# A transformer block with two-pass attention on one core: splits taken from the banks, five units turned by transfers, an update moved to GpSimd

## The chip, the cores and the metric

One NeuronCore of a Trainium2 chip runs the kernel. The metric is the device time of one execution in microseconds, the median of several.

## The reference

Two sequences (batch elements) of 1024 tokens with 256 features. `mod` gives shifts, scales and gates per batch element from a small vector.

```python
h = layernorm(x) * (1 + ca) + sa
Q, K, V = split(h @ c_attn_w + c_attn_b)               # 256 columns each
base = softmax(Q[:, :128] @ K[:, :128].T * 0.25)       # first softmax
ctx  = base @ V[:, :128]
bias = tanh(ctx * cam_gate) @ K[:, :128].T * (0.25 * sigmoid(w0 + 0.5 * w1))
attn = softmax(Q @ K.T * 0.25 + bias)                  # second softmax
x = x + ga * (attn @ V @ c_proj_w + c_proj_b)
h = layernorm(x) * (1 + cb) + sb
x = x + gb * (gelu(h @ proj1.T + b1) @ proj2.T + b2)
```

## The kernel before

Every fp32 product is made of three products of fp32r halves: a value is split into a high half (a copy to fp32r) and a low half (value minus high), and `mm3` (L199 to L203) does high x high, high x low and low x high. So each operand of TensorE costs a high copy and a subtraction, and the engines beside TensorE mostly make these.

The program is written out by hand: each engine has its own list in program order, and semaphores tie them together. An engine that waits holds everything behind it in its list.

For each batch element (b = 0, 1) attention goes in steps s = 0 to 17 over 16 units. A unit is 128 queries against all 1024 keys. Units 0 to 7 are the first softmax, with one 128-row chunk of features (6 matmuls of 512 columns). Units 8 to 15 are the second, with two chunks (12 matmuls). In step s TensorE makes the scores of unit s (`scores`), then turns the probabilities of unit s - 2 (`transpose_probs`, 8 transposes of 128x128, L1305), then does the step's fillers: value and query/key projections in steps 0 to 6, the context product of pair p (`cam_context`, units 2p and 2p + 1) in step 5 + 2p, and from step 11 the product with V (`attend`). Scores alternate between two double banks `s_ps`, so scores of unit u wait for the exp of unit u - 2.

A unit goes: scores; row maximum on VectorE (`row_max`, L904); exp and row sum on ScalarE (`softmax_exp`, L642) into one of three `prob` buffers; reciprocal on VectorE; in the first softmax a division on GpSimd (`divide_by_sum`, L441); the turn into one of two banks `t_ps`; high copy on ScalarE (`prob_high`, L627); low half on VectorE (`prob_low`, L898, pt_lo). The context product of a pair ends in tanh on ScalarE (`cam_tanh`), and `q_update` (L867 to L873, VectorE) adds the scaled tanh to the first query chunk and splits it again. Scores of units 8, 10, 12 and 14 wait for the updates 0, 1, 2 and 3.

Units 8 to 13 (`DMA_UNITS`) are not turned by TensorE. Exp writes them in another order, SyncE writes them to DRAM in four transfers and reads them back in one (a trip: `send_probs`, `write_rows` L349, `read_rows` L356), and VectorE transposes blocks of 32x32 into the bank (`turn_probs`, L882), in step u + 2. Four of the norms make the same trip. SyncE makes trips one after the other, and waits in each for its writes before it issues the read.

Queries and keys come from 8 jobs of 512 tokens (`QK_JOBS`). Each job's bank is copied once by ScalarE to f32s with scale and bias (`qk_bias`), and VectorE makes both halves from there (`qk_split`, L853 and L855), except in the first four jobs of b = 0, where ScalarE makes the high half too.

GpSimd further adds constants and the attention result to x (L459, L465), splits the feed-forward weights in steps 8 to 15 of b = 0 (`split_ffn`, L450), and takes the root for the norms (`inv_std`, L436).

Of the kernel before, what the change touches and what calls it, by code (L numbers as in the profile page):

```python
# [10 lines left out]
P = 128  # L11
# [14 lines left out]
TRIPS = ([("p", 0, u) for u in DMA_UNITS] + [("h", 0, 3), ("h", 1, 0), ("h", 1, 1)]  # L26
         + [("p", 1, u) for u in DMA_UNITS] + [("h", 1, 3)])
# [6 lines left out]
def adaln_block_kernel(nc, x, cols, wmod, w_attn, wv_t, wp, rows, w1_t, w2_t, out):  # L34
# [5 lines left out]
    with ctx:  # L40
# [118 lines left out]
        qk32_ready = lsem("qk32_ready", 8)  # L159
# [15 lines left out]
        qcam_ready = lsem("qcam_ready", T)  # L175
# [16 lines left out]
        probs_back = [sem(f"probs_back{d}") for d in range(2)]  # L192
# [39 lines left out]
        A_READ_OUT = {"v": vlo_ready, "qk": qk32_ready, "ctx": tanh_ready, "pv": o1_ready, "f2": t2_ready,  # L232
                      "wvp": wv_lo_ready, "gate": gate_copied, "row": row_added}

        T_JOBS = []
        for b in range(B):
            T_JOBS += [(b, "h", r) for r in range(4)]
            if b == 0:
                T_JOBS += [(0, "mod", 1)]
            T_JOBS += [(b, "p", n) for n in range(2 * UNITS)] + [(b, "h", r) for r in range(4, 8)]  # L240
# [8 lines left out]
        def read_out(jobs, signals, job):  # L249

            n = jobs.index(job)
            if n < 2:
                return None
            b, kind, k = jobs[n - 2]
            if (b, kind) == (0, "h") and k < 4:
                return hlo_ready, k // 2 * 2 + 2
            if kind == "h":
                return h32_ready, h_count(b, k)
            if kind == "mod":
                return mod_ready, 3  # L260
            s = signals[kind]
            return s, b * per.get(s, 0) + k + 1
# [22 lines left out]
        def slot(trip):  # L285

            d = trip[2] % 2
            same = [t for t in TRIPS[:TRIPS.index(trip) + 1] if t[2] % 2 == d]
            return d, same[-2] if len(same) > 1 else None, len(same)

# [18 lines left out]
        QK_JOBS = [(0, 0), (2, 0), (2, 1), (0, 1), (1, 0), (3, 0), (1, 1), (3, 1)]  # L309

# [3 lines left out]
        def _(sp):  # L314
# [27 lines left out]
            wait(sp, v_psum, 0, T)  # L342
            wait(sp, qk_psum, 0, 8)
            sp.dma_start(w1_raw[:, :, :], w1_t.rearrange("(c p) n -> p c n", p=P)).then_inc(w1_in, 16)
            sp.dma_start(w2_raw[:, :, :], w2_t.rearrange("(c p) n -> p c n", p=P)).then_inc(w2_in, 16)
# [6 lines left out]
            def read_rows(k):  # L352
# [3 lines left out]
                sp.dma_start(quad[:, d, :], turned[k, :, :, :, :].rearrange("q c i n -> (q c) (i n)"))\  # L356
# [12 lines left out]

            def send_norm(b, n):  # L370
# [5 lines left out]
                if kind == "p":  # L376
                    wait(sp, t_psum, ob, 2 * o + 2)
# [4 lines left out]
            for b in range(B):  # L382
                for u in DMA_UNITS:
# [12 lines left out]
        def _(pool):  # L396
# [35 lines left out]
            def inv_std(b, n):  # L432
# [3 lines left out]
                G.tensor_tensor(rstd[:, h], ve[:, h], minus_half[:, :], ALU.pow).then_inc(rstd_ready[n // 2], 1)  # L436

# [77 lines left out]
            for b in range(B):  # L515
                for s in range(UNITS):
                    if s < T:
# [14 lines left out]
                    if s == UNITS - 1:  # L532
                        inv_std(b, 2)
# [20 lines left out]
        def _(act):  # L554
# [43 lines left out]
            def qk_bias(b, j):  # L598
                m, h = QK_JOBS[j]
                wait(act, qk_psum, b, j + 1)  # L600
                if j >= 3:
                    wait(act, qklo_ready, b, j - 2)
                src = s_bank(j) if j < 4 else a_bank(b, "qk", j)[:, :]
                if m < 2:
                    a = A(f32s[:, j % 3, :], src, ACT.Identity, scale=QSCALE, bias=bq_scaled[:, m:m + 1])
                else:
                    a = A(f32s[:, j % 3, :], src, ACT.Identity, bias=cols_sb[:, C_BK + m - 2:C_BK + m - 1])
                a.then_inc(qk32_ready, 1)

            def qk_high(j):  # L610

                m, h = QK_JOBS[j]
                scale, bias = (QSCALE, bq_scaled[:, m:m + 1]) if m < 2 else (1.0, cols_sb[:, C_BK + m - 2:C_BK + m - 1])
                A((q_hi if m < 2 else k_hi)[:, m % 2, h * HALF:(h + 1) * HALF], s_bank(j), ACT.Identity,
                  scale=scale, bias=bias).then_inc(qkhi_ready, 1)
# [4 lines left out]

            def prob_high(b, u):
                for g in range(2):
                    wait(act, t_psum, b, 2 * u + g + 1)
# [7 lines left out]
            def softmax_exp(b, u):  # L631
# [3 lines left out]
                if u - 3 in DMA_UNITS:  # L635
                    act.wait_ge(probs_out, sent("p", b, u - 3))
                elif u >= 3:
                    wait(act, t_psum, b, 2 * (u - 2))
                dst, src = prob[:, u % 3, :], s_ps[u % 2][:, :]
                if u in DMA_UNITS:  # L640
# [37 lines left out]
            qk_bias(0, 0)  # L678
            v_high(0, 0)
            qk_high(0)  # L680
            v_high(0, 1)
            qk_bias(0, 1)
            v_high(0, 2)
            qk_high(1)
# [4 lines left out]
            for b in range(B):  # L689
                if b == 0:  # L690
                    qk_bias(0, 2)
                    qk_high(2)
                    qk_bias(0, 3)
                    qk_high(3)
                    copy_gates()
                else:
                    for j in range(1, 4):
                        qk_bias(b, j)
                        v_high(b, j - 1)
                for s in range(UNITS + 2):  # L700
                    if s - 2 in DMA_UNITS and s < UNITS - 1:
                        softmax_exp(b, s)
                    if s >= 2:
# [5 lines left out]
                    if s < UNITS:  # L709
                        for kind, k in fillers(b, s):  # L710
                            if kind == "v" and s >= 2:
                                v_high(b, k)
                            if kind == "qk":
                                qk_bias(b, k)
# [13 lines left out]
                if b + 1 < B:  # L728
                    qk_bias(b + 1, 0)
# [5 lines left out]
        def _(dve):  # L735
# [43 lines left out]

            def qk_low(j):  # L780
                m, h = QK_JOBS[j]
                hi, lo = (q_hi, q_lo) if m < 2 else (k_hi, k_lo)
                dst = (slice(None), m % 2, slice(h * HALF, (h + 1) * HALF))
                wait(dve, qk32_ready, 0, j + 1)
                wait(dve, qkhi_ready, 0, j + 1)
                V.tensor_tensor(lo[dst], f32s[:, j % 3, :], f(hi[dst]), ALU.subtract).then_inc(qklo_ready, 1)
# [61 lines left out]
            def qk_split(b, j):  # L848
                m, h = QK_JOBS[j]
                hi, lo = (q_hi, q_lo) if m < 2 else (k_hi, k_lo)  # L850
                dst = (slice(None), m % 2, slice(h * HALF, (h + 1) * HALF))
                wait(dve, qk32_ready, b, j + 1)
                V.tensor_copy(hi[dst], f32s[:, j % 3, :]).then_inc(qkhi_ready, 1)  # L853
                wait(dve, qkhi_ready, b, j + 1)
                V.tensor_tensor(lo[dst], f32s[:, j % 3, :], f(hi[dst]), ALU.subtract).then_inc(qklo_ready, 1)  # L855
# [5 lines left out]

            def q_update(b, p):

                dst = (slice(None), 0, slice(2 * P * p, 2 * P * (p + 1)))
                t = th[:, p % 2, :]
                wait(dve, tanh_ready, b, p + 1)
                V.scalar_tensor_tensor(t, t, lw_scaled[:, :], f(q_lo[dst]), ALU.mult, ALU.add).then_inc(qcam_ready, 1)  # L867
                wait(dve, qcam_ready, b, 2 * p + 1)
                V.tensor_tensor(t, t, f(q_hi[dst]), ALU.add).then_inc(qcam_ready, 1)
                wait(dve, qcam_ready, b, 2 * p + 2)  # L870
                V.tensor_copy(q_hi[dst], t).then_inc(qphi_ready, 1)
                wait(dve, qphi_ready, b, p + 1)
                V.tensor_tensor(q_lo[dst], t, f(q_hi[dst]), ALU.subtract).then_inc(qplo_ready, 1)  # L873
# [581 lines left out]
```

## Time and profile before

| | us |
|---|---|
| median of 3 runs (lowest, highest) | 305.36 (304.52, 306.32) |
| the profiled execution, its own time | 304.42 |
| its span | 302.5 |
| TensorE busy in it | 297.4 |
| VectorE, ScalarE, GpSimd busy | 226.3, 157.9, 106.8 |
| transfers | 27.08 MB, mean 90 GB/s |

The span is the time from the first to the last instruction on the engines. Busy times count an instruction from its start to its end. Matmuls are pipelined, so that the duration of one overlaps the next. In the rows, PE is TensorE, DVE VectorE, ACT ScalarE, POOL GpSimd and SPq the queue that SyncE issues transfers to.

### The profile page before, as it was taken

How to read it: one execution, taken by the hardware profiler on the slowest of the kernel's cores; microseconds unless marked ns; L12 is line 12 of the kernel's file. 1: busy time of each engine (PE TensorE's matmuls, PEld its weight loads, DVE VectorE, ACT ScalarE, POOL GpSimd, SP SyncE). 2: the span in 40 equal slices, each digit the busy share in tenths (PEclk: the TensorE clock that was granted, in tenths of full speed). 3: DMA queues.
4: the chain of work that ended last, by engine and by line, in shares of the span. 5: the costliest groups of instructions: out<-in, count | busy, mean ns of one | idle time of the engine just before them, and what ended most of it. 6: DMA issues, size and time to landing. Idle time of an engine off the chain costs nothing.

```text
span 302.5 us, 5086 instructions
## 1 busy us (share of the span) xinstructions
PE 297.4 (98%) x1888; PEld 270.2 (89%) x1888; DVE 226.3 (75%) x448; ACT 157.9 (52%) x268; POOL 106.8 (35%) x130
## 2 busy tenths in 40 slices
PE   8999999999999999999999999999999999999995
PEld 7889888898998988998998888898998999899895
DVE  4796789896899979768964789786889994944521
ACT  2676766463344447617733577554262445923920
POOL 3436743244456548027021141330011344314110
PEclk9999999999999999999999999999999999999999
DMA  6920200726665000451231000005656300141001
GB/s 223 378 96 1 56 17 0 279 69 205 213 194 154 3 0 2 139 175 35 72 106 36 0 2 0 2 0 136 212 161 215 112 1 2 24 134 53 0 20 52
DMA packets 19544, 27.08 MB, mean 90 GB/s; under 512 B 1984, under 2 KB 16064, under 8 KB 19520
## 3 DMA queue, kind: packets, MB, share of 16 engines
q1 hardware_dynamic: 19520, 26.76, 28.2%
q8 instruction: 15, 0.25, 0.3%
q14 instruction: 9, 0.07, 0.1%
HBM read 15.74 MB, written 10.49 MB: 87 GB/s over the span
## 4 chain that ended last, share of the span: by engine, by line
PE 89%; DVE 5%; ACT 2%; issue 2%; POOL 1%; DVEq 0%; POOLq 0%
PE a_ps L203 14%; PE a_ps L201 13%; PE a_ps L202 13%; PE s_ps L201 12%; PE s_ps L203 12%; PE s_ps L202 12%; PE t_ps L1305 5%; PE s_ps L1134 2%; DVE nmax L904 2%; DVE pt_lo L898 1%; ACT prob L642 1%; PE t_ps L1230 1%; ACT pt_hi L627 1%; PE s_ps L1160 1%; PE s_ps L1169 1%
## 5 line engine op out<-in xcount | busy, mean ns | idle before, releaser
L642 ACT ACTIVATE prob<-s_ps,nmax 128x1024 f32<-128x1024 f32 x32 | 35.8, 1118 | 48.4 <-DVE nmax L904 48.3
L904 DVE TENSOR_REDUCE nmax<-s_ps 128x1 f32<-128x1024 f32 x32 | 38.9, 1217 | 11.8 <-PE s_ps L203 11.6
L627 ACT ACTIVATE pt_hi<-t_ps 128x512 fp32r<-128x512 f32 x64 | 34.9, 595 | 23.9 <-PE t_ps L1305 19.4
L898 DVE TENSOR_TENSOR pt_lo<-t_ps,pt_hi 128x512 fp32r<-128x512 f32 x64 | 41.0, 683 | 3.8 <-ACT pt_hi L627 3.7
L201 PE MATMUL s_ps<-k_hi,q_hi 128*128 128x512 f32 x96 | 38.0, 396 | 0.0
L203 PE MATMUL s_ps<-k_hi,q_lo 128*128 128x512 f32 x96 | 37.6, 392 | 0.0
L202 PE MATMUL s_ps<-k_lo,q_hi 128*128 128x512 f32 x96 | 37.5, 391 | 0.0
L201 PE MATMUL a_ps<-v_hi,pt_hi 128*128 128x256 f32 x128 | 36.4, 284 | 0.0
L203 PE MATMUL a_ps<-w_hi,pt_lo 128*128 128x256 f32 x128 | 36.2, 283 | 0.0
L201 PE MATMUL a_ps<-w_hi,pt_hi 128*128 128x256 f32 x128 | 36.2, 283 | 0.0
L202 PE MATMUL a_ps<-w_lo,pt_hi 128*128 128x256 f32 x128 | 36.2, 283 | 0.0
L203 PE MATMUL a_ps<-v_hi,pt_lo 128*128 128x256 f32 x128 | 35.8, 280 | 0.0
L202 PE MATMUL a_ps<-v_lo,pt_hi 128*128 128x256 f32 x128 | 35.8, 279 | 0.0
L441 POOL TENSOR_SCALAR prob<-prob,rinv 128x1024 f32<-128x1024 f32 x16 | 18.3, 1145 | 48.8 <-DVE rinv L908 48.7
L933 DVE TENSOR_TENSOR pt_lo<-prob,pt_hi 128x512 fp32r<-128x512 f32 x32 | 23.3, 753 | 11.5 <-ACT pt_hi L665 11.4
L306 POOL TENSOR_TENSOR x_all<-x_all,o 128x256 f32<-128x256 f32 x15 | 11.1, 739 | 55.9 <-DVE o L928 55.9
L465 POOL TENSOR_TENSOR x_all<-x_all,o 128x256 f32<-128x256 f32 x16 | 11.8, 738 | 49.6 <-DVE o L919 49.6
L662 ACT ACTIVATE prob<-s_ps,cols_sb 128x512 f32<-128x512 f32 x32 | 22.0, 687 | 13.4 <-PE s_ps L203 13.3
L201 PE MATMUL s_ps<-ht_hi,w_hi 128*128 128x512 f32 x64 | 25.1, 392 | 0.0
L202 PE MATMUL s_ps<-ht_lo,w_hi 128*128 128x512 f32 x64 | 24.9, 390 | 0.0
L203 PE MATMUL s_ps<-ht_hi,w_lo 128*128 128x512 f32 x64 | 24.9, 389 | 0.0
L202 PEld LDWEIGHTS a_ps<-w_lo,pt_hi 128*128 128x128 f32 x128 | 24.6, 192 | 0.2
(166 smaller groups left out, 756.3 us busy)
## 6 DMA issues: line engine op xcount, KB each, us to landing
f32s<-turned SPq DMA_DIRECT2D x16, 512.0 KB, 3.5
turned<-prob SPq DMA_DIRECT2D x48, 128.0 KB, 2.9
w_raw<-w_t SPq DMA_DIRECT2D x2, 1024.0 KB, 6.2
turned<-xn SPq DMA_DIRECT2D x16, 128.0 KB, 2.4
out<-x_all SPq DMA_DIRECT2D x16, 128.0 KB, 1.7
x_all<-x SPq DMA_DIRECT2D x3, 512.0 KB, 10.0
wmod_raw<-wmod SPq DMA_DIRECT2D x1, 1024.0 KB, 8.8
wmod_raw<-wmod SPq DMA_DIRECT2D x2, 256.0 KB, 4.6
```

Of the source, the lines that this page charges most:

```text
L201: nc.tensor.matmul(o, st_hi, mv_hi, start=first, stop=False)
L202: nc.tensor.matmul(o, st_hi, mv_lo, start=False, stop=False)
L203: return nc.tensor.matmul(o, st_lo, mv_hi, start=False, stop=last)
L441: G.tensor_scalar(prob[:, u % 3, :], prob[:, u % 3, :], rinv[:, u:u + 1], 1.0, ALU.mult, ALU.mult).then_inc(pnorm_ready, 1)
L465: G.tensor_tensor(xt, xt, o1[:, t % 2, :], ALU.add).then_inc(x2_ready, 1)
L627: A(pt_hi[:, (u // 2) % 2, 4 * g:4 * g + 4, (u % 2) * P:(u % 2 + 1) * P], t_bank(b, "p", 2 * u + g)[:, :].rearrange("p (t n) -> p t n", n= ...
L642: A(dst, src, ACT.Exp, bias=nmax[:, u:u + 1], accum_out=rsum[:, u:u + 1]).then_inc(exp_ready, 1)
L662: A(gelu_of(n), s_bank(n % 4), ACT.Gelu, bias=cols_sb[:, C_B1 + n % HC:C_B1 + n % HC + 1]).then_inc(gelu_ready, 1)
L898: V.tensor_tensor(pt_lo[dst], t_bank(b, "p", 2 * u + g)[:, :].rearrange("p (t n) -> p t n", n=P), f(pt_hi[dst]), ALU.subtract).then_inc(pt ...
L904: V.tensor_reduce(nmax[:, u:u + 1], s_ps[u % 2][:, :], AX.X, ALU.max, negate=True).then_inc(nmax_ready, 1)
L933: V.tensor_tensor(gt_lo[:, n % HC, :], gelu_of(n), f(gt_hi[:, n % HC, :]), ALU.subtract)\
L1305: last = nc.tensor.transpose(t_bank(b, "p", 2 * u + g)[:, t * P:(t + 1) * P], prob[:, u % 3, c:c + P], ident[:, :])
```

## The change

- `by_dma`, `DMA_CAM`: units 4 and 6 of b = 0 and 2, 4 and 6 of b = 1 of the first softmax make the trip too, after their division. They land in xn, and VectorE's turn, the high copy and the low half come at the end of step u + 3. The order in which units go through the turning banks changes accordingly (`turn_order`: 5 before 4, 7 before 6, 3 before 2).
- `qk_copies`, `qk_low`: ScalarE makes the high half of every job straight from the bank. For queries it also makes the fp32 copy, from which VectorE takes the low half; for keys VectorE takes the low half straight from the bank (`scalar_tensor_tensor`: bank + bias - high). No high copy is left on VectorE.
- `q_update` runs on GpSimd, as five instructions, ahead of the division of its step.
- The two loads of the feed-forward weights are issued by ScalarE in step 6 of b = 0 (`load_ffn`), not by SyncE.
- In step 15 GpSimd takes the root (`inv_std(b, 2)`) before its two additions, not after.

```diff
+DMA_CAM = ((4, 6), (2, 4, 6))
+TRIPS = ([("p", 0, u) for u in (*DMA_CAM[0], *DMA_UNITS)] + [("h", 0, 3), ("h", 1, 0), ("h", 1, 1)]
+         + [("p", 1, u) for u in (*DMA_CAM[1], *DMA_UNITS)] + [("h", 1, 3)])
...
+        def turn_order(b):
+            order = list(range(UNITS))
+            for u in DMA_CAM[b]:
+                order[u], order[u + 1] = u + 1, u
+            return order
...
+        def landing(d):
+            return xn[:, :, :].rearrange("p t e -> p (t e)") if d == 2 else quad[:, d, :]
...
             def send_probs(b, u):
                 k = TRIPS.index(("p", b, u))
-                wait(sp, exp_ready, b, u + 1)
+                wait(sp, pnorm_ready if u < T else exp_ready, b, u + 1)
                 write_rows(k, prob[:, u % 3, :])
-                if u - 2 in DMA_UNITS:
-                    wait(sp, t_psum, b, 2 * (u - 2) + 2)
-                else:
+                if by_dma(b, u - 2) and u not in (T, T + 1):
+                    wait(sp, t_psum, b, turned_by(b, u - 2))
+                elif u >= T:
                     wait(sp, qklo_ready, b, 8)
+                elif b == 0:
+                    wait(sp, ht_psum, 0, 4)
                 read_rows(k)
...
+            def q_update(b, p):
+                dst = (slice(None), 0, slice(2 * P * p, 2 * P * (p + 1)))
+                t = th[:, p % 2, :]
+                wait(pool, tanh_ready, b, p + 1)
+                G.tensor_scalar(t, t, lw_scaled[:, :], 1.0, ALU.mult, ALU.mult).then_inc(qcam_ready, 1)
+                wait(pool, qcam_ready, b, 3 * p + 1)
+                G.tensor_tensor(t, t, f(q_lo[dst]), ALU.add).then_inc(qcam_ready, 1)
+                wait(pool, qcam_ready, b, 3 * p + 2)
+                G.tensor_tensor(t, t, f(q_hi[dst]), ALU.add).then_inc(qcam_ready, 1)
+                wait(pool, qcam_ready, b, 3 * p + 3)
+                G.tensor_scalar(q_hi[dst], t, 1.0, 1.0, ALU.mult, ALU.mult).then_inc(qphi_ready, 1)
+                wait(pool, qphi_ready, b, p + 1)
+                G.tensor_tensor(q_lo[dst], t, f(q_hi[dst]), ALU.subtract).then_inc(qplo_ready, 1)
...
                 for s in range(UNITS):
+                    for kind, p in fillers(b, s - 1):
+                        if kind == "ctx":
+                            q_update(b, p)
                     if s < T:
                         divide_by_sum(b, s)
...
+                    if s == UNITS - 1:
+                        inv_std(b, 2)
                     if s >= 10:
                         attn_const(b, s - 10)
                     if s >= 11:
                         attn_residual(b, s - 11)
-                    if s == UNITS - 1:
-                        inv_std(b, 2)
...
+            def qk_copies(b, j):
                 m, h = QK_JOBS[j]
                 wait(act, qk_psum, b, j + 1)
                 src = s_bank(j) if j < 4 else a_bank(b, "qk", j)[:, :]
+                dst = (slice(None), m % 2, slice(h * HALF, (h + 1) * HALF))
                 if m < 2:
+                    if j >= 3:
+                        wait(act, qklo_ready, b, j - 2)
+                    A(f32s[:, j % 3, :], src, ACT.Identity, scale=QSCALE, bias=bq_scaled[:, m:m + 1]).then_inc(q32_ready, 1)
+                    A(q_hi[dst], src, ACT.Identity, scale=QSCALE, bias=bq_scaled[:, m:m + 1]).then_inc(qkhi_ready, 1)
                 else:
+                    A(k_hi[dst], src, ACT.Identity, bias=cols_sb[:, C_BK + m - 2:C_BK + m - 1]).then_inc(qkhi_ready, 1)
...
                 for s in range(UNITS + 2):
                     if s - 2 in DMA_UNITS and s < UNITS - 1:
                         softmax_exp(b, s)
-                    if s >= 2:
+                    if s >= 2 and not (s - 2 < T and by_dma(b, s - 2)):
                         prob_high(b, s - 2)
...
+                    if b == 0 and s == 6:
+                        load_ffn()
+                    if s - 3 < T and by_dma(b, s - 3):
+                        prob_high(b, s - 3)
...
+            def qk_low(b, j):
                 m, h = QK_JOBS[j]
                 dst = (slice(None), m % 2, slice(h * HALF, (h + 1) * HALF))
                 wait(dve, qkhi_ready, b, j + 1)
+                if m < 2:
+                    wait(dve, q32_ready, b, Q_JOBS.index(j) + 1)
+                    V.tensor_tensor(q_lo[dst], f32s[:, j % 3, :], f(q_hi[dst]), ALU.subtract).then_inc(qklo_ready, 1)
+                else:
+                    src = s_bank(j) if j < 4 else a_bank(b, "qk", j)[:, :]
+                    V.scalar_tensor_tensor(k_lo[dst], src, cols_sb[:, C_BK + m - 2:C_BK + m - 1], f(k_hi[dst]),
+                                           ALU.add, ALU.subtract).then_inc(qklo_ready, 1)
...
-                    for kind, k in fillers(b, s - 1):
-                        if kind == "ctx":
-                            q_update(b, k)
...
+                    if s - 3 < T and by_dma(b, s - 3):
+                        turn_probs(b, s - 3)
+                        prob_low(b, s - 3)
...
-                    if s >= 2 and s - 2 not in DMA_UNITS:
+                    if s >= 2 and not by_dma(b, s - 2):
                         transpose_probs(b, s - 2)
```

## Rows read from the trace of the kernel before

**Rows 1.** The page's first part: busy us, share of the span, instructions.
```profile
PE 297.4 (98%) x1888; PEld 270.2 (89%) x1888; DVE 226.3 (75%) x448; ACT 157.9 (52%) x268; POOL 106.8 (35%) x130
```

**Rows 2.** Waits of PE: us in total, times, longest.
```profile
PE t_ps L1230 <- DVE pt_lo L898: 0.6, 1, 0.6
```

**Rows 3.** Windows: us, busy (instructions), clock, transfers; then chain: start, us, what.
```profile
67.78:109.40 41.62, 41.03 (x282) 37.76 (x281) 35.04 (x69) 16.57 (x32) 22.70 (x27) 1.00 0.45 140
...
81.81 1.24 DVE nmax L904
```

**Rows 4.** The chain, step 7 of the first element.
```profile
54.36 0.87 PE t_ps L1305 x8
```

**Rows 5.** Lines by form: shapes, count, busy us, mean ns, idle before.
```profile
L1305 PE MATMUL t_ps<-ident,prob 128*128 128x128 f32 x160 | 20.7, 273 | 0.0
...
L882 DVE STREAM_TRANSPOSE t_ps<-f32s 128x512 f32<-128x512 f32 x32 | 21.0, 701 | 0.0
...
L853 DVE CAST q_hi<-f32s 128x512 fp32r<-128x512 f32 x6 | 4.0, 664 | 2.3 <-ACT f32s L605 2.3
...
L459 POOL TENSOR_TENSOR x_all<-x_all,consts 128x256 f32<-128x256 f32 x16 | 11.8, 737 | 0.0
...
L450 POOL TENSOR_SCALAR w_hi<-w_raw 128x512 fp32r<-128x512 f32 x8 | 5.0, 620 | 16.2 <-DVE nmax L904 16.2
```

**Rows 6.** SyncE's queue: start, us, issue; then part 6: median us to landing.
```profile
53.48 0.47 SPq L345 DMA_DIRECT2D w_raw<-w_t  x1
63.39 1.80 SPq L349 DMA_DIRECT2D turned<-prob  x4
67.18 0.34 SPq L356 DMA_DIRECT2D f32s<-turned  x1
...
f32s<-turned SPq DMA_DIRECT2D x16, 512.0 KB, 3.5
```

**Rows 7.** Timeline, steps 6 and 7 of the first element.
```profile
49.35 0.56 ACT L649 ACTIVATE th<-a_ps,gate_bias,cols_sb 128x256 f32<-128x256 f32 x1 [0.52 <-PE a_ps L203]
...
53.64 1.28 POOL L441 TENSOR_SCALAR prob<-prob,rinv 128x1024 f32<-128x1024 f32 x1 [3.98 <-DVE rinv L908]
53.97 1.23 DVE L869 TENSOR_TENSOR th<-th,q_hi 128x256 f32<-128x256 f32 x1
```

**Rows 8.** Windows (PE, PEld, DVE, ACT, POOL) from score start to score start: steps 6, 7, 9, 10.
```profile
49.15:52.81 3.66, 3.66 (x23) 3.09 (x21) 3.56 (x5) 2.20 (x4) 0.52 (x1) 1.00 0.00 0
52.81:57.81 5.00, 5.00 (x40) 4.69 (x38) 4.64 (x9) 2.21 (x5) 1.28 (x1) 1.00 0.67 246
...
61.34:67.78 6.44, 6.44 (x47) 5.91 (x46) 6.11 (x11) 4.13 (x7) 2.79 (x4) 1.00 0.32 81
67.78:70.52 2.74, 2.74 (x15) 2.26 (x14) 0.31 (x2) 0.75 (x3) 1.03 (x1) 1.00 0.82 257
```

**Rows 9.** One query update's window, DVE on th alone; then the tile view (min/median/max ns).
```profile
216.50:218.40 1.90, 1.62 (x4) 1.00 0.90 284
...
L869 DVE TENSOR_TENSOR th<-th,q_hi x8: 424/426/1241, 54.0 to 228.2; 128x256 f32<-128x256 f32 x8
```

**Rows 10.** Timeline, steps 14 to 17 of the first element.
```profile
92.50 0.39 PE L203 MATMUL s_ps<-k_hi,q_lo 128*128 128x512 f32 x1
...
93.27 1.21 DVE L904 TENSOR_REDUCE nmax<-s_ps 128x1 f32<-128x1024 f32 x1
...
103.14 0.94 DVE L816 TENSOR_SCALAR ve<-mv 128x4 f32<-128x4 f32 x1
103.99 1.28 DVE L898 TENSOR_TENSOR pt_lo<-t_ps,pt_hi 128x512 fp32r<-128x512 f32 x2
...
104.71 0.73 POOL L465 TENSOR_TENSOR x_all<-x_all,o 128x256 f32<-128x256 f32 x1
105.40 1.04 POOL L436 TENSOR_TENSOR rstd<-ve,minus_half 128x4 f32<-128x4 f32 x1
106.48 1.80 DVE L835 TENSOR_SCALAR xn<-x_all,mv,rstd 128x256 f32<-128x256 f32 x4 [1.14 <-POOL rstd L436]
108.53 0.28 PE L203 MATMUL a_ps<-v_hi,pt_lo 128*128 128x256 f32 x1
109.42 0.30 PE L1230 MATMUL t_ps<-ident,xn 128*128 128x128 f32 x1 [0.61 <-DVE pt_lo L898]
```

More of the change, by code:

```diff
@@ L191, in adaln_block_kernel @@
         probs_out = sem("probs_out")
-        probs_back = [sem(f"probs_back{d}") for d in range(2)]
+        probs_back = [sem(f"probs_back{d}") for d in range(3)]
         def wait(eng, s, it, k):
@@ L239, in adaln_block_kernel @@
                 T_JOBS += [(0, "mod", 1)]
-            T_JOBS += [(b, "p", n) for n in range(2 * UNITS)] + [(b, "h", r) for r in range(4, 8)]
+            T_JOBS += [(b, "p", 2 * u + g) for u in turn_order(b) for g in range(2)] + [(b, "h", r) for r in range(4, 8)]
         T_READ_OUT = {"p": ptlo_ready}
@@ L261, in read_out @@
             s = signals[kind]
-            return s, b * per.get(s, 0) + k + 1
+            if kind == "qk" and QK_JOBS[k][0] >= 2:
+                s = qklo_ready
+            return s, b * per.get(s, 0) + (turned_by(b, k // 2, k % 2) if kind == "p" else k + 1)
         def v_bank(b, t):
@@ L285, in slot, with home, by_dma @@
         def slot(trip):
-            d = trip[2] % 2
-            same = [t for t in TRIPS[:TRIPS.index(trip) + 1] if t[2] % 2 == d]
+            def home(t):
+                return 2 if t[0] == "p" and t[2] < T else t[2] % 2
+            d = home(trip)
+            same = [t for t in TRIPS[:TRIPS.index(trip) + 1] if home(t) == d]
             return d, same[-2] if len(same) > 1 else None, len(same)
+        def by_dma(b, u):
+            return ("p", b, u) in TRIPS
+        def landing(d):
+            return xn[:, :, :].rearrange("p t e -> p (t e)") if d == 2 else quad[:, d, :]
         def gelu_of(n):
@@ L309, in adaln_block_kernel @@
         QK_JOBS = [(0, 0), (2, 0), (2, 1), (0, 1), (1, 0), (3, 0), (1, 1), (3, 1)]
+        Q_JOBS = [j for j in range(8) if QK_JOBS[j][0] < 2]
         block = ctx.enter_context(nc.Block())
@@ L355, in read_rows @@
                 sp.wait_ge(probs_out, 16 * Q * (k + 1))
-                sp.dma_start(quad[:, d, :], turned[k, :, :, :, :].rearrange("q c i n -> (q c) (i n)"))\
+                sp.dma_start(landing(d), turned[k, :, :, :, :].rearrange("q c i n -> (q c) (i n)"))\
                     .then_inc(probs_back[d], 16)
@@ L376, in send_norm @@
                 if kind == "p":
-                    wait(sp, t_psum, ob, 2 * o + 2)
+                    wait(sp, t_psum, ob, turned_by(ob, o))
                 else:
@@ L382, in _ @@
             for b in range(B):
-                for u in DMA_UNITS:
+                for u in (*DMA_CAM[b], *DMA_UNITS):
                     send_probs(b, u)
@@ L619, in v_high, with load_ffn @@
                 A(v_hi[:, t, :], v_bank(b, t)[:, 0:NV], ACT.Copy).then_inc(vhi_ready, 1)
+            def load_ffn():
+                wait(act, v_psum, 0, T)
+                wait(act, qk_psum, 0, 8)
+                nc.scalar.dma_start(w1_raw[:, :, :], w1_t.rearrange("(c p) n -> p c n", p=P)).then_inc(w1_in, 16)
+                nc.scalar.dma_start(w2_raw[:, :, :], w2_t.rearrange("(c p) n -> p c n", p=P)).then_inc(w2_in, 16)
             def prob_high(b, u):
                 for g in range(2):
-                    wait(act, t_psum, b, 2 * u + g + 1)
+                    wait(act, t_psum, b, turned_by(b, u, g))
                     if b == 0 and u == 0:
@@ L690, in _ @@
                 if b == 0:
[L691 to L694, printed above, removed]
+                    qk_copies(0, 2)
+                    qk_copies(0, 3)
                     copy_gates()
@@ L778, in h_low @@
                 V.tensor_tensor(ht_lo[dst], h32[:, r % 2, :], f(ht_hi[dst]), ALU.subtract).then_inc(hlo_ready, 1)
[L780 to L786, printed above, removed]
             def norm_stats(b, n):
@@ L860, in v_low @@
                     .then_inc(vlo_ready, 1)
[L862 to L873, printed above, removed]
             def turn(trip, kind, jobs, signal):
@@ L895, in prob_low @@
                 for g in range(2):
-                    wait(dve, pthi_ready, b, 2 * u + g + 1)
+                    wait(dve, pthi_ready, b, turned_by(b, u, g))
                     dst = (slice(None), (u // 2) % 2, slice(4 * g, 4 * g + 4), slice((u % 2) * P, (u % 2 + 1) * P))
@@ L1011, in _ @@
                         tile_stats(b, TH - 1)
-                    if s >= 2:
+                    if s >= 2 and not (s - 2 < T and by_dma(b, s - 2)):
                         prob_low(b, s - 2)
@@ L1281, in scores @@
                 if u == 1:
-                    wait(pe, qk32_ready if b else qkhi_ready, b, 4)
+                    wait(pe, qkhi_ready, b, 4)
                 if u >= 2:
```

64 lines of the change are left out of this document (21 added, 43 removed).

## The prediction

> **What bounds the kernel now.** First the page's busy times: TensorE is busy 297.4 of a span of 302.5 us, VectorE 75% [rows 1]. A share of 98% could still hide small bubbles, so next come TensorE's own waits: beside the first operand there is one, 0.6 us on VectorE's pt_lo [rows 2]. Apart from that wait, the start and the tail, the kernel goes as fast as TensorE takes its list. An edit is worth what it takes off that list, plus what it takes off that wait, minus new waits; work saved on the other engines is worth nothing in itself. The chain of waits seems to say otherwise, since it runs through VectorE and ScalarE from 81.8 to 109 us. But it is followed back from that one wait, and shows that this stretch has little room, not that it costs 27 us: TensorE is busy 41.03 of its 41.62 us, at its full 2.4 GHz [rows 3].
>
> **Term 1, five units by transfers.** TensorE turns a unit's probabilities with 8 transposes. The line view's mean of 273 ns for one [rows 5] is not the price, since matmuls overlap; the chain gives start to start 0.87 us for all 8 [rows 4], 109 ns each. Units 4 and 6 of the first batch element and 2, 4 and 6 of the second leave the list: 5 x 0.87 = 4.35 us. No other matmul is added, removed or reshaped, so this is gained in full unless a wait appears.
>
> Elsewhere it adds 5 x 2 block transposes of 0.70 us on VectorE [rows 5], 7.0 us in all, and 20 writes and 5 reads on SyncE. ScalarE's and VectorE's copies of such a unit stay, and come one step later. Is a turned unit there when it is wanted? A trip took 3.8 us from the first write's issue to the read's (63.39 to 67.18), and a read lands in 3.5 us [rows 6]: 7.3 us. Take unit 6 of the first element. Its division ran from 53.64 for 1.28 us [rows 7], so it is back at 62.2. Its turn stands at the end of step 9, which began at 61.34 [rows 8] and, with two pieces of 0.87 us gone before it, begins at 59.6. Scores 2.8 us (step 10, which is nothing else [rows 8]), row maximum 1.2 and the pt_lo of unit 7 1.3 [rows 10] put the turn at 64.9: 2.7 us in hand. The same count gives some 1.6 us for unit 6 of the second element, more for the others. A late trip holds VectorE at the turn, with the next row maximum behind it, then that unit's exp, then the scores two units on: some 4 us more pass before TensorE waits. I take 0, from 0 (nothing that TensorE waits for today gets faster by it) to 2 us lost.
>
> The steps also get shorter, and VectorE has least room in them: busy 3.56 of 3.66 us in step 6, 4.64 of 5.00 in step 7, 6.11 of 6.44 in step 9 [rows 8]. In step 6 it loses a pt_lo (1.3), the query update (1.62 [rows 9]) and the high copy (0.4 to 0.7), and keeps row maximum, reciprocal and one low half: 2.1 us in a step of 2.8. Step 7 then has a row maximum, two units' pt_lo, a turn and a reciprocal: 5.3 against 5.0, behind 0.7 to spare. Step 9 has the same 5.3 against 6.4. In all VectorE gets 7.0 us and loses 8 x 1.62 = 13.0 and 12 high copies, six of which took 4.0 [rows 5]. No stall from there.
>
> **Keys and queries straight from the banks.** Six query jobs get a second ScalarE copy and two key jobs lose one, some 0.7 us each. ScalarE's fullest step is step 5 of the second element: two units' high copies (4 x 0.6), exp (1.3), two query copies (1.4) and tanh (0.56 [rows 7]) make 5.7 us, against a TensorE step of 6.4. Keys free their bank with VectorE's low half, about 0.8 us later than now; the context product that waits for such a bank has scores, transposes and another job ahead of it, over 3 us. I take 0, from 0 to 0.3 lost. At the start TensorE has no wait that this could shorten.
>
> **Query update on GpSimd.** Three tensor_tensor on 128x256 at 737 ns, and two tensor_scalar, which I put at half of the 128x512 form's 620 [rows 5]: 2.8 us, 3.1 with gaps, where VectorE took 1.62 [rows 9]. Update 0 starts when tanh ends, at 49.9 [rows 7] or 0.2 later for the extra copy, and scores of unit 8 want it at the start of step 8, 57.81 [rows 8] less 0.87: 6.8 us for 3.1. Update 1 has about 8 us, 2 and 3 some ten. Behind update 0 on GpSimd stands the division of unit 6, whose sum is ready at 53.6 today, as the update ends; behind updates 2 and 3 the splits of the feed-forward weights and two additions, 3.4 us in a step of 5.5. I take 0, up to 1 us lost.
>
> A rule of the Trainium skill speaks against this move (SBUF — State Buffer, "Who interferes with whom"): a VectorE instruction with two SBUF inputs and a GpSimd instruction that reads SBUF block each other, the second one waiting the first one out. The trace agrees: the update's addition took 1.23 us beside a division on GpSimd [rows 7], against a median of 0.43 [rows 9]. By that rule 25 us more of GpSimd could block VectorE; but most of what VectorE does in these steps has one input in a bank, and its pt_lo kept 1.28 us for two beside GpSimd's additions [rows 10]. The queries' low half alone is left, so by the rule too the sum would stay.
>
> **Feed-forward weights issued by ScalarE.** Two issues of 0.4 to 0.5 us [rows 6] enter its step 6, where it was busy 2.20 of 3.66 [rows 8]; 1.1 us of copies leave that step. The loads start when they did, but now run beside unit 6's trip. If both its legs took twice as long, that would eat the 2.7 us and some of the 4 behind them. 0, up to 1.
>
> **Term 2, the root moved up.** Near the end of the first element's attention VectorE idles 1.14 us for the root, then applies the norm (1.80), the gate, and only then makes the pt_lo for which TensorE waits until 109.42. The root's input was ready at 104.08 (103.14 + 0.94), yet it ran at 105.40, behind two additions [rows 10]. Ahead of them it ends at 105.1, before VectorE is through with its reciprocal at 105.3, and VectorE gains 1.1 us. TensorE's bubble is 0.89 us from start to start where 0.12 is the pace: 0.77 [rows 10]. What is late next: from the row maximum at 93.27 to 109.42 are 16.15 us, less 1.1 is 15.05; TensorE needs from the end of that unit's scores (92.50 + 0.39) to 108.65 15.76. 0.7 us in hand, so the whole bubble goes. I take 0.75, from 0 to 0.77. The second element has no such wait.
>
> **Sum.** The profiled execution took 304.42 us for its span of 302.5. 304.42 - 4.35 - 0.75 = 299.3; it was 0.94 us under the median of 305.36, so the median should be 300.3.
>
> **The rivals.** (B) The transposes go, but the wait at 109 stays or another of its size takes its place: 305.36 - 4.35 = 301.0. For it the gapless chain of 27 us, against it the 0.7 us in hand and an update fewer on VectorE. (C) Late trips: beside the weights, or in SyncE's queue, where every trip is made in order and units 8 to 13 come next. TensorE then waits 0.5 to 1 us in two to four places: 2.5 given back, 302.8. Against it the 1.6 to 2.7 us in hand and the 4 behind. (D) Slower: the update on GpSimd is too late for the scores of units 8 and 10, the one new wait of TensorE on GpSimd. It decides from 6.8 us for update 0 and 8.4 for update 1. At 10 us an update TensorE waits 3.2 + 1.6 in each element, 9.6 in all: 309.9. Against it: that is three times what the nearest rows give; for it, only that no GpSimd row is of just this kind.
>
> **How the numbers follow.** Forecast 0.72, B 0.12, C 0.12, D 0.04. The range takes in B and C, and below it a median that comes out as low beside the forecast as the lowest of the three runs was beside theirs (0.84): 299.3 to 302.9. No change can be told from 0.5%, 1.5 us: faster means below 303.8. The forecast, B and nearly all of C lie there: faster 0.92, same 0.04, slower 0.04.
>
> **What would show it.** Right: 120 TensorE transposes of prob instead of 160, 42 VectorE block transposes instead of 32, TensorE busy about 293 us, and no wait of it at 107 to 108; VectorE not idle ahead of unit 6's turn; scores of units 8 and 10 at TensorE's pace. Wrong: TensorE waits of over 1 us in steps 5 to 12 of either element, or matmuls at another pace.

## The result: 1.8 us faster, not 5

| | us |
|---|---|
| before, median of 8 runs (lowest, highest) | 305.14 (304.24, 306.32) |
| after, median of 8 runs | 303.30 (302.18, 304.39) |
| ratio | 0.9936, interval 0.9909 to 0.9963 |
| the profiled execution after, its span | 303.96, 302.1 |

The change is faster, but by 1.8 us instead of the 5 that were forecast, and the time lies outside the range (299.3 to 302.9). TensorE's list did become as short as foreseen. The first fence is the page's first part after, the second its line for TensorE's transposes of prob, the third TensorE's waits.

```profile
PE 293.6 (97%) x1848; PEld 264.9 (88%) x1848; DVE 213.6 (71%) x414; ACT 163.0 (54%) x272; POOL 131.0 (43%) x170
```

```profile
L1332 PE MATMUL t_ps<-ident,prob 128*128 128x128 f32 x120 | 16.0, 275 | 2.7 <-DVE pt_lo L925 2.7
```

```profile
PE t_ps L1332 <- DVE pt_lo L925: 2.7, 4, 1.1
...
PE a_ps L202 <- DVE pt_lo L925: 0.3, 1, 0.3
PE t_ps L1257 <- DVE pt_lo L925: 0.2, 1, 0.2
```

Against [rows 1, 2, 5]: 40 transposes fewer, TensorE busy 3.8 us less, and where one wait of 0.6 us stood there are now six, 3.2 us in all. These are idle times; waits at the very start are left out, since unit 0's scores start at 24.21 in both kernels. From start to start, as the prediction measured the bubble at 109 (0.77), the bubbles after are 0.22, 1.23, 0.61 and 0.36 us in the first batch element and 0.43, 1.10 and 0.35 in the second: 4.30 us. So the span's account is -4.35 (transposes) - 0.77 (the old bubble) + 4.30 (the new ones) = -0.8, and it fell by 0.4. The profiled execution after lies 0.7 us above its median and the one before 0.7 under its own; that is why the spans differ by less than the medians.

What those waits hang on is seen in VectorE's turns. The fence is VectorE's timeline after, first element, the turns of units 6, 8, 9, 10, 11, 12 and 13 (start, us, in brackets the idle time before and what ended it).

```profile
65.72 1.32 DVE L909 STREAM_TRANSPOSE t_ps<-xn 128x512 f32<-128x512 f32 x2 [0.29 <-DMA xn<-turned]
...
71.41 1.32 DVE L909 STREAM_TRANSPOSE t_ps<-f32s 128x512 f32<-128x512 f32 x2 [1.23 <-DMA f32s<-turned]
...
76.78 1.32 DVE L909 STREAM_TRANSPOSE t_ps<-f32s 128x512 f32<-128x512 f32 x2 [1.56 <-DMA f32s<-turned]
...
81.88 1.32 DVE L909 STREAM_TRANSPOSE t_ps<-f32s 128x512 f32<-128x512 f32 x2 [0.60 <-DMA f32s<-turned]
...
88.44 1.32 DVE L909 STREAM_TRANSPOSE t_ps<-f32s 128x512 f32<-128x512 f32 x2 [1.62 <-DMA f32s<-turned]
...
93.72 1.32 DVE L909 STREAM_TRANSPOSE t_ps<-f32s 128x512 f32<-128x512 f32 x2 [0.75 <-DMA f32s<-turned]
...
98.59 1.32 DVE L909 STREAM_TRANSPOSE t_ps<-f32s 128x512 f32<-128x512 f32 x2 [1.46 <-DMA f32s<-turned]
```

Every turn of units 8 to 13 waits for its landing, 14.2 us in all over both elements; before, none did (the L882 row in [rows 5] has 0.0 idle). Unit 13 was turned at 98.17 before and is turned at 98.59 now. From there the way to the largest wait is short: the landing at 98.57, the turn, the copies of unit 13 (pt_lo from 99.98), and only then a free bank for TensorE's transposes of unit 14, at 100.82 after 1.08 us idle. TensorE had come 1.74 us ahead by step 9, had given back 0.22 of it when unit 13 was turned, and 2.42 by 109 us, which is the whole lead and most of what the old bubble was. Why the landings are late is read from SyncE's queue after, same stretch.

```profile
54.59 1.76 SPq L371 DMA_DIRECT2D turned<-prob  x4
62.22 0.34 SPq L378 DMA_DIRECT2D xn<-turned  x1
62.61 2.44 SPq L371 DMA_DIRECT2D turned<-prob  x4
67.61 0.34 SPq L378 DMA_DIRECT2D f32s<-turned  x1
67.99 1.91 SPq L371 DMA_DIRECT2D turned<-prob  x4
72.86 0.34 SPq L378 DMA_DIRECT2D f32s<-turned  x1
73.25 1.90 SPq L371 DMA_DIRECT2D turned<-prob  x4
78.11 0.34 SPq L378 DMA_DIRECT2D f32s<-turned  x1
```

Two things differ from [rows 6]. Unit 6's writes took until 62.22 (they landed 6.3 us after issue, beside the weights' 2 MB) and its read then ran beside unit 8's writes, which needed 5.0 us from first issue to read instead of 3.8. From there each trip follows the one before with no gap, every 5.2 to 5.4 us (6.5 for unit 11): the next unit's exp is done 1.8 to 2.8 us before SyncE comes to it. Before, each trip in this element began as its exp ended. SyncE's queue, with its wait for each trip's writes in front of the next trip, has become what sets the pace. The chain of waits after says the same: 27% of it is SyncE's queue and transfers, and from 54 to 98 us in the first element it holds nothing else but one turn of VectorE, at 76.78.

### The profile page after: what moved, and what is told of

It is laid out like the page before. It is cut to its first block, busy times and chain, and to the rows that moved or that the text cites. A ratio compares the mean times of both kernels' runs of the same rounds, so it can differ in the third digit from the quotient of the medians.

```text
span 302.1 us, 5045 instructions
## 1 busy us (share of the span) xinstructions
PE 293.6 (97%) x1848; PEld 264.9 (88%) x1848; DVE 213.6 (71%) x414; ACT 163.0 (54%) x272; POOL 131.0 (43%) x170
## 4 chain that ended last, share of the span: by engine, by line
PE 55%; DMA 20%; DVE 9%; SPq 7%; ACT 4%; issue 2%; POOL 1%; DVEq 0%
DMA turned<-prob 15%; PE a_ps L204 8%; PE a_ps L202 8%; PE a_ps L203 8%; PE s_ps L202 7%; PE s_ps L203 7%; PE s_ps L204 7%; SPq L371 5%; DMA f32s<-turned 4%; DVE nmax L931 3%; DVE pt_lo L925 2%; PE t_ps L1332 2%; ACT prob L686 2%; DMA wmod_raw<-wmod 2%; DVE t_ps L909 1%
## 5 line engine op out<-in xcount | busy, mean ns | idle before, releaser
L671 ACT ACTIVATE pt_hi<-t_ps 128x512 fp32r<-128x512 f32 x64 | 36.5, 598 | 22.2 <-DVE t_ps L909 14.5
L909 DVE STREAM_TRANSPOSE t_ps<-f32s 128x512 f32<-128x512 f32 x32 | 21.1, 705 | 14.2 <-DMA f32s<-turned 14.2
L202 PEld LDWEIGHTS a_ps<-v_hi,pt_hi 128*128 128x128 f32 x128 | 24.0, 187 | 1.4 <-DVE pt_lo L925 1.2
```

The lines of the kernel that those rows point to most:

```text
L202: nc.tensor.matmul(o, st_hi, mv_hi, start=first, stop=False)
L671: A(pt_hi[:, (u // 2) % 2, 4 * g:4 * g + 4, (u % 2) * P:(u % 2 + 1) * P], t_bank(b, "p", 2 * u + g)[:, :].rearrange("p (t n) -> p t n", n= ...
L909: V.transpose(t_bank(trip[1], kind, jobs[g])[:, :].rearrange("p (a i c) -> p i a c", a=TH, i=Q), landing(d).rearrange("p (i g a r) -> p g ...
```

## The experiments

Theory T: the trips in SyncE's queue bind. Rivals: R1, the update on GpSimd or the second query copy on ScalarE makes the waits; R2, the transfer engines' load, not the order in the queue; R3, the weights' load beside unit 6's trip. Medians are given with the ratio to the kernel before on the same chip. A median alone tells differences under about 1 us badly, so small ones are read from the traces.

**Root alone** (the kernel before).

```diff
+                    if s == UNITS - 1:
+                        inv_std(b, 2)
                     if s >= 10:
                         attn_const(b, s - 10)
                     if s >= 11:
                         attn_residual(b, s - 11)
-                    if s == UNITS - 1:
-                        inv_std(b, 2)
```

> The kernel before with one edit: the root of step 15 is taken ahead of GpSimd's two additions. Theory T (the trips of units 8 to 13, one after the other in SyncE's queue, hold the changed kernel): in the kernel before they do not bind, so TensorE's wait near 109 goes and the time falls by about 0.75 us, to 304.4. Rival R1 (something else, of the order of the root's wait, stands right behind it): no fall, 305.1.

Measured: 305.04, ratio 0.998 (0.9957 to 1.0003): the 304.4 under T was missed, and no gain can be told from none. The bubble at 108.3 shrank from 0.77 to 0.37 us, it did not go. VectorE's and GpSimd's timelines of this kernel:

```profile
105.08 2.61 DVE L835 TENSOR_SCALAR xn<-x_all,mv,rstd 128x256 f32<-128x256 f32 x4
```

```profile
103.97 1.05 POOL L436 TENSOR_TENSOR rstd<-ve,minus_half 128x4 f32<-128x4 f32 x1
104.99 0.73 POOL L459 TENSOR_TENSOR x_all<-x_all,consts 128x256 f32<-128x256 f32 x1
105.67 0.79 POOL L465 TENSOR_TENSOR x_all<-x_all,o 128x256 f32<-128x256 f32 x1
106.42 0.80 POOL L459 TENSOR_TENSOR x_all<-x_all,consts 128x256 f32<-128x256 f32 x1
```

The norm starts 1.4 us earlier than in [rows 10], as it should, but takes 2.61 us instead of 1.80: the additions that the root was moved past now run beside it. In the second element, where there was no wait to win, the norm takes 2.35 us instead of 1.37. That element also has two bubbles that the kernel before has not, 0.64 and 0.35 us. They have another cause: unit 13's trip needed 5.5 us from first write to read (3.7 before), and its turn waited 1.38 us for the landing.

```profile
240.72 1.32 DVE L882 STREAM_TRANSPOSE t_ps<-f32s 128x512 f32<-128x512 f32 x2 [1.38 <-DMA f32s<-turned]
```

So the row of six trips has little to spare even with no trip added.

**No first-softmax unit by transfer.**

```diff
-DMA_CAM = ((4, 6), (2, 4, 6))
+DMA_CAM = ((), ())
```

> The changed kernel with no unit of the first softmax by transfer: TensorE turns all five again. Theory T: TensorE's list is 4.35 us longer, but the 4.3 us of new waits in steps 13 to 17 go, since TensorE no longer runs ahead of the trips and SyncE's queue is free when unit 8's exp is done; 304.4, that is the kernel before less the root's wait. Rival R1 (the update on GpSimd, or the second query copy on ScalarE, makes the waits): the waits stay and the transposes come on top, 307 to 308.

Measured: 304.26, ratio 0.9954 (0.9932 to 0.9976). VectorE waits 1.3 us for landings instead of 14.2, and TensorE's bubbles in both elements together are 0.9 us. R1 falls: with the update on GpSimd and all the copies on ScalarE the waits are gone, but for 1.15 us at unit 13's turn in the second element, as with the root alone.

**Unit 13 by TensorE.**

```diff
-DMA_UNITS = range(T, UNITS - 2)
+DMA_UNITS = range(T, UNITS - 3)
```

> The changed kernel with unit 13 of both elements turned by TensorE, so that the row of trips is one shorter. Theory T: TensorE's list is 1.74 us longer, but turn 13, which came latest, is gone and most of the 4.3 us of waits with it: 301 to 302. Rival R1: the waits stay, 305.0.

Measured: 301.08, ratio 0.9862 (0.9824 to 0.9900). 16 more transposes on TensorE (1.74 us), and the kernel is 2.2 us faster. After its first operand TensorE has no wait in the list at all. The lateness is bound to the last trip: the turns of units 8 to 12 still wait for landings (8.1 us in all), but no turn follows in step 15, and the row maximum there starts 2.3 us after its scores (2.2 before, over 4 after).

**Unit 9's writes ahead** (with two semaphores, so that a read waits for its own writes alone).

```diff
...
                 for u in (*DMA_CAM[b], *DMA_UNITS):
-                    send_probs(b, u)
+                    if u != T + 1:
+                        write_probs(b, u)
+                    if u == T:
+                        write_probs(b, u + 1)
+                    read_probs(b, u)
```

> The changed kernel in which SyncE issues the writes of unit 9 before it waits for unit 8's writes and issues its read (two semaphores, so that each read waits for its own writes). Unit 9's exp was done about 2 us before its writes were issued, so unit 9's read and all trips behind it should come 1.5 us earlier. Theory T: the waits of 4.3 us fall by about 1.5 us in each element, 300.5 to 301.5. Rival R1: 303.3. Rival R2 (the trips bind by the load of the transfer engines, not by their order in the queue): writes and reads only share the same engines differently, 303.

Measured: 300.37, ratio 0.9833 (0.9786 to 0.9881). Same trips, same bytes, same engines; only SyncE does not stand and wait for unit 8's writes while unit 9 is ready. Its queue in the first element:

```profile
63.47 4.46 SPq L372 DMA_DIRECT2D turned<-prob  x8
68.28 2.42 SPq L379 DMA_DIRECT2D f32s<-turned  x2
72.09 2.16 SPq L372 DMA_DIRECT2D turned<-prob  x4
```

Unit 10's writes start at 72.09 instead of 73.25, in a run whose scores began 0.6 us later (24.81 against 24.21). VectorE waits 3.6 us for landings instead of 14.2; TensorE has bubbles of 0.36 and 0.64 us left. R2 falls as the main cause, and T stands. R1 falls here once more, with the trips in place.

**The second load of weights later** (the changed kernel).

```diff
-                nc.scalar.dma_start(w2_raw[:, :, :], w2_t.rearrange("(c p) n -> p c n", p=P)).then_inc(w2_in, 16)
...
                     send_probs(b, u)
+                    if (b, u) == (0, 6):
+                        wait(sp, v_psum, 0, T)
+                        wait(sp, qk_psum, 0, 8)
+                        sp.dma_start(w2_raw[:, :, :], w2_t.rearrange("(c p) n -> p c n", p=P)).then_inc(w2_in, 16)
```

> The changed kernel, with the second load of feed-forward weights issued by SyncE right behind unit 6's read in the first element, so that the writes of unit 6 share the transfer engines with one load instead of two. Writes of unit 6 landed 6.3 us after their issue in the changed kernel against 3.4 for the others; now 3 to 4. Theory T (the pace of the trips, each 5.3 us, and not the one slow trip): unit 8's writes start only 0.3 us earlier, at its exp, so the waits fall by no more than 0.3: 303.0. Rival R3 (the load beside unit 6's trip starts the lateness): the first element's 2.4 us of waits go, 300.9.

Measured: 304.49, ratio 0.9974 (0.9944 to 1.0005), above both values that were expected. Unit 6's writes landed 2.9 us after issue instead of 6.3, its read was issued at 58.75 instead of 62.22, and still:

```profile
62.39 1.77 SPq L371 DMA_DIRECT2D turned<-prob  x4
68.14 0.34 SPq L378 DMA_DIRECT2D f32s<-turned  x1
68.52 1.88 SPq L371 DMA_DIRECT2D turned<-prob  x4
```

The load only moved: now it runs beside unit 8's writes, which need 5.75 us. Bubbles in the first element: 0.46, 0.23, 1.18, 0.61, 0.36. Taking one load away from unit 6 does not help: unit 8's writes start only 0.2 us earlier, at its exp. R3 as the whole cause falls also by the second element of the changed kernel, which has no such load, where unit 8's trip took 3.7 us as before, and which has 1.9 us of new bubbles all the same. What the first element would gain with the load where it meets neither unit 6 nor unit 8 was not tried.

**Root back** (unit 9's writes ahead; the edit of the first experiment the other way round).

```diff
-                    if s == UNITS - 1:
-                        inv_std(b, 2)
                     if s >= 10:
...
                         attn_residual(b, s - 11)
+                    if s == UNITS - 1:
+                        inv_std(b, 2)
```

> The kernel with unit 9's writes ahead (300.37 us), with the root put back behind the two additions. If the root's move is worth its 0.75 us, TensorE's wait at the end of the first element's attention is 0.9 us or more and the time 301.1. If the move gains only what the norm does not lose again (in the kernel with the root alone moved the norm's four instructions took 2.61 us beside GpSimd's additions instead of 1.80, and 0.37 us of bubble stayed), the wait is 0.7 to 0.8 and the time 300.8.

Measured: 300.18, ratio 0.9844 (0.9818 to 0.9870). The bubble at that place is 0.56 us, with the root moved it is 0.36: worth 0.2 us here. Both expected times (301.1 and 300.8) were missed: with the root back the kernel is no slower than with it moved (300.37).

**Update on VectorE** (unit 9's writes ahead; the update as it was before the change).

```diff
...
-                    for kind, p in fillers(b, s - 1):
-                        if kind == "ctx":
-                            q_update(b, p)
                     if s < T:
                         divide_by_sum(b, s)
...
                         row_recip(b, s - 1)
+                    for kind, k in fillers(b, s - 1):
+                        if kind == "ctx":
+                            q_update(b, k)
```

> The kernel with unit 9's writes ahead, with the query update back on VectorE as in the kernel before (four instructions, 1.62 us). If VectorE's room in steps 7 to 9 is what the added turns use up, the row maxima of units 8 and 9 come 1 to 1.6 us later, the trips behind them too, and TensorE waits 1 to 2 us more in each element: 302.5 to 304. If VectorE had room enough, as the prediction's count of each step said before the update left it, no change: 300.4.

Measured: 308.83, ratio 1.0122 (1.0090 to 1.0154): 8.5 us slower than the same kernel with the update on GpSimd, far past what I expected. VectorE's timeline in the first element, steps 6 to 8:

```profile
53.50 0.16 DVE L938 RECIPROCAL rinv<-rsum 128x1 f32<-128x1 f32 x1 [1.27 <-ACT prob L676]
53.58 0.47 DVE L897 SCALAR_TENSOR_TENSOR th<-th,lw_scaled,q_lo 128x256 f32<-128x256 f32 x1
54.08 1.22 DVE L899 TENSOR_TENSOR th<-th,q_hi 128x256 f32<-128x256 f32 x1
...
56.67 1.21 DVE L934 TENSOR_REDUCE nmax<-s_ps 128x1 f32<-128x1024 f32 x1
...
61.83 1.22 DVE L934 TENSOR_REDUCE nmax<-s_ps 128x1 f32<-128x1024 f32 x1
```

The update stands behind a reciprocal that waits 1.27 us for an exp, so the row maximum of unit 7 starts at 56.67 (54.42 in the changed kernel), unit 8's at 61.83 (59.88), and unit 8's trip and turn behind them. At unit 8's product with V TensorE then idles 2.46 us, and pays a second time, as the windows of this kernel show (us, busy of PE, PEld, DVE, ACT, POOL, granted clock, transfers; the last two are the same place in the second element):

```profile
75.00:78.00 3.00, 0.54 (x5) 0.34 (x4) 2.89 (x6) 1.19 (x2) 0.74 (x2) 1.00 0.79 251
78.00:80.00 2.00, 2.00 (x11) 2.00 (x12) 1.90 (x5) 0.00 (x0) 0.00 (x0) 0.53 0.12 39
80.00:82.00 2.00, 2.00 (x13) 2.00 (x13) 1.93 (x4) 1.43 (x3) 1.29 (x2) 0.61 0.66 223
82.00:84.00 2.00, 2.00 (x12) 1.72 (x12) 1.68 (x3) 1.21 (x3) 1.33 (x2) 1.00 0.68 167
...
219.00:223.00 4.00, 1.28 (x11) 1.08 (x10) 3.29 (x7) 1.19 (x2) 0.00 (x0) 1.00 0.73 242
223.00:226.00 3.00, 3.00 (x25) 2.87 (x25) 2.93 (x6) 0.86 (x1) 0.00 (x0) 1.00 0.46 168
```

After the first idle stretch the granted clock is 0.53 and 0.61 in two windows, that is 3.4 us at the lower level of 1.2 GHz. After the one in the second element, 2.72 us and so even longer, it stayed at 1.00; no run here tells why. Start to start, TensorE's bubbles in this run come to 7.7 us against 1.0 in the run with the update on GpSimd, and 3.4 us at half the clock lose 1.7: together 8.4 of the 8.5.

**Additions after the norm** (unit 9's writes ahead).

```diff
                     if s == UNITS - 1:
                         inv_std(b, 2)
+                        wait(pool, xn_ready, b, 3)
```

> The kernel with unit 9's writes ahead, with GpSimd's additions of step 15 made to wait for the norm. The norm's four instructions should take 1.8 us instead of 2.61, the pt_lo behind them comes 0.8 us earlier, and the last 0.36 us of bubble at the end of the first element's attention goes: 300.0. If the 2.61 us have nothing to do with GpSimd, they stay and the time with them, 300.4.

Measured: 300.32, ratio 0.9851 (0.9826 to 0.9876), no change in time. What made the norm longer is shown, though. This is VectorE's norm without a GpSimd instruction beside it:

```profile
103.48 1.36 DVE L880 TENSOR_SCALAR xn<-x_all,mv,rstd 128x256 f32<-128x256 f32 x4
```

1.36 us instead of 2.61. The bubble ahead of the norm's transposes is gone, and one of 0.53 us came at 110.7, where the feed-forward part waits for the low half of h: the additions now run beside VectorE's high copy of h, which took 0.89 us instead of 0.47.

**Transposes left out** (the changed kernel with no unit of the first softmax by transfer; it leaves out 6 of TensorE's 8 transposes of each of those five units).

```diff
-DMA_CAM = ((4, 6), (2, 4, 6))
+DMA_CAM = ((), ())
...
-                    for t in range(4):
+                    for t in range(3 if (b, u) in ((0, 4), (0, 6), (1, 2), (1, 4), (1, 6)) else 0, 4):
```

> The changed kernel with no first-softmax unit by transfer, and with 6 of the 8 TensorE transposes of those five units left out (their probabilities are wrong). TensorE's list is 3.3 us shorter than in the kernel without them left out (304.26) and no trip is added. Theory T in its strict form (the six trips of units 8 to 13 have a pace of 5.3 us of their own, and any lead of TensorE runs into it): VectorE waits for landings 5 us or more in all instead of 1.3, TensorE has 1 to 1.5 us of new waits, 302 to 302.5. Rival T' (the added trips are what makes SyncE late): VectorE's waits for landings stay near 1.3 us, the 3.3 us are gained in full, 301.0.

Measured: 301.47, ratio 0.9871 (0.9827 to 0.9915). VectorE waits 1.9 us for landings, TensorE's bubbles are 0.60 and 0.36 us. A lead of TensorE by itself is kept for the most part: 2.8 of 3.3 us, 2.5 by the two ratios. So T's strict form falls (the six trips do not bind by themselves at this lead), and T' stands: what comes with the added trips makes SyncE late. TensorE's lead was smaller here (1.3 and 2.0 us in the two elements instead of 1.7 and 2.6), and VectorE was spared the added turns too, so this run does not part the trips from those.

**The changed kernel and the write-ahead once more, on one chip.**

> The changed kernel once more, as it is, on the same chip as the kernel with unit 9's writes ahead: 303.3, as before.

> The kernel with unit 9's writes ahead once more, on the same chip as the changed kernel: 300.4, and 2.5 to 3 us less than the changed kernel. If the difference were one between chips, it would be under 1 us here.

Measured: 303.79 (ratio 0.9938, 0.9911 to 0.9966) and 299.39 (0.9806, 0.9772 to 0.9840), 4.4 us apart. The kernel with unit 9's writes ahead beats both kernels: 5 to 6 us under before, where the prediction wanted the change to be. The changed kernel again has bubbles of some 4 us; with unit 9's writes ahead there are two of 0.13 us.

## Why the prediction was wrong

**Term 1, the size: right.** 40 transposes at 109 ns from the chain are 4.35 us. With the queue mended the kernel gains 5 to 6 us, and with 30 transposes (3.27 us) left out and nothing added it gained 2.5 to 2.8.

**The step that failed: "I take 0" for the trips.** The runs showed 4.3 us of new bubbles in its place (0.36 of them is what term 2 left), behind turns that waited 14.2 us for their landings. With nothing changed but the order of the writes in SyncE's queue, 1.0 us of bubbles was left, and 0.26 in the second run of that kernel. The working asked one question of a trip: is this unit back when its turn comes. It never asked what the trip does to the units behind it in SyncE's queue, though it named units 8 to 13 as next in it. The numbers were at hand. The 3.8 us of [rows 6] are unit 8's, the shortest but one of the six; those of units 9 to 12 beside the last one's read took 4.2 to 4.7 from first write to read. And the turns of the kernel before show how little a landing could slip:

```profile
71.86 1.31 DVE L882 STREAM_TRANSPOSE t_ps<-f32s 128x512 f32<-128x512 f32 x2
...
82.96 1.31 DVE L882 STREAM_TRANSPOSE t_ps<-f32s 128x512 f32<-128x512 f32 x2
...
98.17 1.30 DVE L882 STREAM_TRANSPOSE t_ps<-f32s 128x512 f32<-128x512 f32 x2
```

Units 8, 10 and 13 had landed at 70.88, 82.07 and 97.73: 0.98, 0.89 and 0.44 us ahead (unit 9 1.29, units 11 and 12 over 2.4). TensorE's own lead of 1.7 to 2.6 us moves every want forward by more than that, and the queue did not follow: the six landings after lie between 0.2 us earlier and 2.0 us later than before. A row of trips that starts late and takes 5.2 to 5.4 us each gains at most 0.3 a trip on steps of 5.5. Rival C had this mechanism at 302.8 and a chance of 0.12; the measured 303.3 is C plus half a microsecond. It was put too low because its bound rested on slack counted for the moved units only. The sign of being wrong looked for the waits in steps 5 to 12; they came in steps 14 to 17.

**The margin of unit 6.** "Back at 62.2, wanted at 64.9." The writes were issued at 54.59, as worked out, but the read only at 62.22, and the turn waited 0.29 us, until 65.72. The landing came 3.5 us later than worked out, beside the weights' load; the prediction had this case and said that it would eat the margin.

**VectorE's room.** "No stall from there" held, but only with the update gone. The count of busy time per step missed that VectorE waits in its list for an exp, with the update behind it. So the sentence that work saved on other engines is worth nothing in itself does not hold for this kernel: put back, the update costs 8.5 us. In the second element the turn of unit 4 held the row maximum of unit 8 to 201.88, 1.1 us past its scores, and that trip's start with it.

**Term 2: 0.75 was 0.2 to 0.4 at its place, and nothing that the times can tell.** The root came earlier by 1.4 us, and the norm behind it became 0.8 us longer. The rule that the prediction quoted was weighed for the update only, not for the instruction that this term was about. The trace of before had a sign of it: its four norm instructions took 1.80 us in the first element, with an addition beside the first of them, and 1.37 in the second, where the addition ended 0.12 us in.

**Update on GpSimd: right.** Its five instructions took 3.11 us and 3.44 with gaps (3.1 foreseen), all in time. The two tensor_scalar took 0.48 and 0.41 us, not 0.31. Rival D did not happen. **Straight splits: nothing lost, as foreseen** (304.26 with all of them and no trips, against 305.04 with the root alone; the intervals overlap). **B** was half right: new waits in the same place, from another cause.

**Left open.** In the second element the late start is smaller, and part of its 1.9 us comes from unit 11's trip: the last of its writes landed 5.5 us after issue (220.36 to 225.83), those of its neighbours 3.3 to 3.4. The same unit is slow in the first element (4.6) and in the second run of the changed kernel, not in the kernel before; with unit 9's writes ahead it is not always slow. The traces show one thing beside it, a packet of 16 KB in a queue of its own (page, part 3, of the changed kernel for 223 to 225 us):

```profile
q8 instruction: 1, 0.02, 3.0%
```

It ran from 223.39 to 224.35, between the last write's issue and its landing, and so did one at 82.12 in the first element, and at 235.32 in the run with the root alone, where unit 13 was slow. No run moved these packets, so this is a coincidence worth testing and not a cause.

## What to carry to other kernels

When work moves to a transfer, count the issuing queue like an engine: time per trip with the wait inside it, the order, and who stands behind. If the queue waits for one transfer's end with another's data ready, issue the second first, with a semaphore of its own. And a saving on the bounding engine moves every other deadline forward by as much, so a margin must be counted against the new times of all that follows, not only of what was moved.

## What the runs showed of the hardware

- Four VectorE tensor_scalar on 128x256 fp32, SBUF to SBUF, took 1.36 us alone, 1.80 with one GpSimd addition and 2.61 with several beside them; single ones about 400 ns against 789 to 831 (root alone and before). The Trainium skill (SBUF — State Buffer, "Who interferes with whom") states that copy, cast and tensor_scalar can enter two-port modes, and that in these VectorE and GpSimd block each other; the longer times agree, the mode itself is in no trace.
- An idle stretch of TensorE of 2.46 us was followed by 3.4 us at the lower clock (0.53 and 0.61 granted in two windows of 2 us); one of 2.72 us in the same execution was not, and the clock stayed at 1.00. In the changed kernel, with idle stretches up to 1.08 us, the clock stayed at 1.00 in those stretches.
- Writes of 128 KB landed 2.4 us after issue with nothing large beside them (unit 8, before the change), 3.4 beside a 512 KB read, and 6.3 beside 2 MB of loads issued from ScalarE.
